# Attention on one Trainium2 core: value products in groups of four key tiles, one ring of three PSUM banks

## The reference

```python
h = relu(layernorm(x)); x = x + (adj @ h) @ W0 + b0
h = relu(layernorm(x)); x = x + norm_adj @ (h @ W1) + b1
h = relu(layernorm(x)); x = x + L2(h, mask = adj)     # attention, projection, o + layernorm(o)
h = relu(layernorm(x)); x = x + L3(h, mask = adj)     # attention, projection

def attention(h, mask):                 # for each of 8 heads of width 32
    s = scale * q @ k.T                 # 1024 x 1024
    p = softmax(where(mask, s, -inf))   # L3 adds -1e9 in place of -inf
    return (p @ v) @ Wo + bo
```

## Time and profile before

| | us |
|---|---|
| median of 3 runs | 2976.08 (2975.07 to 2977.13) |
| the profiled execution | 2974.42 |
| its span, first to last instruction | 2972.6 |

### The profile page before, as it was taken

The page is one execution under the profiler, slowest core; times in us unless marked ns, Lnnn a source line. Parts: engine busy times, 40 slices in busy tenths (PEclk is TensorE's granted clock), DMA queues, the critical chain, the costliest instruction groups (busy, mean ns, idle before and its releaser), DMA issues.

```text
span 2972.6 us, 59755 instructions
## 1 busy us (share of the span) xinstructions
PE 2906.1 (98%) x23872; PEld 2199.0 (74%) x23872; DVE 2401.1 (81%) x4427; ACT 2126.1 (72%) x3794; POOL 591.3 (20%) x538
## 2 busy tenths in 40 slices
PE   7999997999999999999999989999999999999998
PEld 6888886777777777777777767777777777777776
DVE  6776775879888888888888878888888787878786
ACT  3000002888888888888888878888888888888887
POOL 2222220105050504131322323010101010101000
PEclk9999998999999999999999999999999999999999
DMA  3001003323233233232323252323233332323232
GB/s 124 29 29 58 29 29 94 70 56 90 69 83 75 71 74 83 65 93 61 96 51 97 67 140 68 90 66 85 65 81 74 82 76 72 87 55 93 65 75 58
DMA packets 123588, 217.19 MB, mean 73 GB/s; under 512 B 20016, under 2 KB 88240, under 8 KB 123312
## 3 DMA queue, kind: packets, MB, share of 16 engines
q1 hardware_dynamic: 122160, 209.14, 28.4%
q0 software_dynamic: 1152, 4.19, 0.6%
HBM read 53.87 MB, written 25.17 MB: 27 GB/s over the span
## 4 chain that ended last, share of the span: by engine, by line
PE 79%; ACT 2%; DVE 1%; DMA 1%; issue 0%; ACTq 0%; DVEq 0%
PE t_pt_ps L732 32%; PE t_ot_ps L751 17%; PE t_s_ps L720 15%; PE t_g_ps L705 4%; PE t_g_ps L706 4%; PE t_g_ps L707 4%; PE t_g_ps L772 1%; PE t_g_ps L776 1%; PE t_g_ps L791 1%; ACT t_T L870 1%; ACT t_PT L875 1%; DMA mask<-in_adj 1%; DVE t_st_lo L957 0%; ACT t_st_hi L860 0%; ACT t_ot L881 0%
## 5 line engine op out<-in xcount | busy, mean ns | idle before, releaser
L939 DVE CUSTOM_DVE_ANT_0 t_T<-t_s_ps,mask 128x1024 f32<-128x1024 f32 x1024 | 1240.6, 1215 | 117.3 <-PE t_s_ps L720 112.5
L870 ACT ACTIVATE t_T<-t_T,t_low 128x1024 f32<-128x1024 f32 x1024 | 1178.8, 1151 | 43.1 <-DVE t_low L939 37.9
L732 PEld LDWEIGHTS t_pt_ps<-t_ident,t_T 128*128 128x128 f32 x8192 | 885.2, 141 | 325.7 <-issue 279.5
L732 PE MATMUL t_pt_ps<-t_ident,t_T 128*128 128x128 f32 x8192 | 1112.6, 279 | 6.3 <-DVE t_PT L1014 4.5
L875 ACT ACTIVATE t_PT<-t_pt_ps 128x512 f32<-128x512 f32 x1324 | 755.9, 596 | 317.9 <-PE t_pt_ps L732 306.7
L720 PE MATMUL t_s_ps<-t_k,t_q 128*128 128x512 f32 x2048 | 729.7, 437 | 8.3 <-DMA t_k<-t_st_lo 7.1
L1014 DVE COPY t_PT<-t_pt_ps 128x512 f32<-128x512 f32 x724 | 499.1, 689 | 196.6 <-PE t_pt_ps L732 194.0
L751 PE MATMUL t_ot_ps<-t_PT,shared 128*32 128x256 f32 x8192 | 549.4, 386 | 8.1 <-ACT t_PT L875 7.9
L751 PEld LDWEIGHTS t_ot_ps<-t_PT,shared 128*32 128x32 f32 x8192 | 215.1, 109 | 255.4 <-issue 128.0
L247 ACT ACTIVATE g_yT_hi<-g_ps 128x512 fp32r<-128x512 f32 x64 | 38.3, 598 | 400.5 <-PE g_ps L187 400.5
L720 PEld LDWEIGHTS t_s_ps<-t_k,t_q 128*128 128x128 f32 x2048 | 310.6, 192 | 9.3 <-DMA t_k<-t_st_lo 7.6
(11 more groups left out here) (185 smaller groups left out, 3158.1 us busy)
## 6 DMA issues: line engine op xcount, KB each, us to landing
t_q<-t_st_hi SPq DMA_DIRECT2D x256, 128.0 KB, 2.3
t_k<-t_st_hi SPq DMA_DIRECT2D x256, 128.0 KB, 2.4
t_k<-t_st_lo SPq DMA_DIRECT2D x256, 128.0 KB, 2.4
t_q<-t_st_lo SPq DMA_DIRECT2D x256, 128.0 KB, 2.4
shared<-x_after_graph_layers SPq DMA_DIRECT2D x8, 1024.0 KB, 6.5
t_xe<-x_after_graph_layers SPq DMA_DIRECT2D x32, 256.0 KB, 3.1
x_after_layer<-t_xe SPq DMA_DIRECT2D x32, 256.0 KB, 2.1
shared<-x_after_layer SPq DMA_DIRECT2D x8, 1024.0 KB, 6.8
```

Source lines behind the costliest of these rows:

```text
L732: last = nc.tensor.transpose(pt_ps[half][:, i * P:(i + 1) * P], T[u % RING][:, kt * P:(kt + 1) * P], ident[:])
L870: nc.scalar.activation(T[u % RING][:], T[u % RING][:], ACT.Exp, bias=low[:, u % RING:u % RING + 1], scale=-1.0, accum_out=rsum[:, u:u + 1] ...
L939: nc.vector.tensor_tensor_reduce(out=T[u % RING][:], in0=s_ps[u % 2][:], in1=mask[:, qt, :], scale=1.0, scalar=3.4e38, op0=ALU.add, op1=AL ...
```

## The change

- GROUP is 4: the value products of four key tiles follow each other, once in four units.
- The two banks for transposes and the one for blocks become one ring of three (`ring_ps`). `bank_plan` walks through the order in which TensorE fills banks, gives the fills (each half of a unit's transposes, each block) to banks 0, 1, 2, 0 ... and notes for each the bank and its count there. Each bank has a semaphore for filled and one for emptied; each fill waits for the emptying of the fill three before.
- All three engines' loops go over four units at a time, with an order written out. The halves of a unit's transposes are separate steps, partly half 1 first.
- The blocks stand in other units; ScalarE copies both halves in the 27 units of `BOTH_ON_ACT`.
- `mask3` of a tile is done just ahead of the first `masked` that uses it.
- SP's store of pair 1 stands behind the load of head 4, pair 2 behind head 5, pair 3 behind head 6.

```diff
-GROUP = 2
-EARLY = [(9, ("norm", 3)), (11, ("turn", 0)), (13, ("out", 0)), (15, ("turn", 1)), (17, ("out", 1)),
+GROUP = 4
+EARLY = [(10, ("norm", 3)), (13, ("turn", 0)), (16, ("out", 0)), (19, ("turn", 1)), (24, ("out", 1)),
          (26, ("turn", 2)), (28, ("out", 2)), (30, ("turn", 3)), (32, ("out", 3))]
-MID = [(18, ("qk", 1, 0, 0)), (20, ("qk", 1, 1, 0)), (22, ("qk", 1, 0, 1)), (24, ("qk", 1, 1, 1)),
-       (33, ("norm", 0)), (49, ("norm", 1)), (60, ("norm", 2))]
-NEXT = [(35, ("h", 0, 0)), (37, ("h", 0, 1)), (40, ("h", 1, 0)), (42, ("h", 1, 1)),
-        (44, ("v", 0)), (45, ("v", 1)), (47, ("v", 2)), (48, ("v", 3)),
-        (51, ("qk", 0, 0, 0)), (53, ("qk", 0, 1, 0)), (54, ("qk", 0, 0, 1)), (56, ("qk", 0, 1, 1))]
+MID = [(17, ("qk", 1, 0, 0)), (18, ("qk", 1, 1, 0)), (21, ("qk", 1, 0, 1)), (22, ("qk", 1, 1, 1)),
+       (34, ("norm", 0)), (43, ("norm", 1)), (59, ("norm", 2))]
+NEXT = [(35, ("h", 0, 0)), (37, ("h", 0, 1)), (38, ("h", 1, 0)), (39, ("h", 1, 1)),
+        (40, ("v", 0)), (44, ("v", 1)), (46, ("v", 2)), (47, ("v", 3)),
+        (49, ("qk", 0, 0, 0)), (50, ("qk", 0, 1, 0)), (51, ("qk", 0, 0, 1)), (53, ("qk", 0, 1, 1))]
+BOTH_ON_ACT = {2, 6, 11, 15, 17, 18, 19, 22, 23, 25, 26, 27, 30, 31, 33, 34, 35, 39, 42, 43, 45, 46, 47, 54, 55, 58, 62}
...
+def bank_plan(n_jobs):
...
+        for u in range(0, UNITS, GROUP):
+            order = [("T", job, u, 1), ("T", job, u, 0), ("T", job, u + 1, 0), ("T", job, u + 1, 1), ("B", job, u),
+                     ("T", job, u + 2, 1), ("T", job, u + 2, 0), ("B", job, u + 1), ("T", job, u + 3, 0), ("B", job, u + 2),
+                     ("T", job, u + 3, 1), ("B", job, u + 3)]
+            for key in order:
+                if key[0] == "T" or key[2] in table:
+                    use(key, n % BANKS)
+                    n += 1
...
         @block.tensor
...
+            def transposes(job, u, half):
+
+                if half == (1, 0, 1, 0)[u % GROUP]:
+                    pe.wait_ge(p_done, UNITS * job + u + 1)
+                b, n = place["T", job, u, half]
+                if n:
+                    pe.wait_ge(bank_freed[b], n)
...
-                for u in range(UNITS):
-                    if u + 2 < UNITS or after is not None:
-                        scores(job, u + 2, UNITS * job + u + 1)
...
-                    if u % GROUP == 0 and (u >= NT or before is not None):
+                for u in range(0, UNITS, GROUP):
+                    scores(job, u + 2)
+                    if u >= NT or before is not None:
                         for w in range(u, u + GROUP):
                             values(job, w)
-                    transposes(job, u)
+                    transposes(job, u, 1)
+                    scores(job, u + 3)
+                    transposes(job, u, 0)
+                    transposes(job, u + 1, 0)
+                    transposes(job, u + 1, 1)
+                    scores(job, u + 4)
+                    block_of(u)
+                    transposes(job, u + 2, 1)
+                    transposes(job, u + 2, 0)
+                    block_of(u + 1)
+                    scores(job, u + 5)
+                    transposes(job, u + 3, 0)
+                    block_of(u + 2)
+                    transposes(job, u + 3, 1)
+                    block_of(u + 3)
...
         @block.scalar
...
+                for u in range(0, UNITS, GROUP):
+                    exp(job, u + 1)
+                    if u % (2 * NT) == NT - GROUP and (u >= NT or before is not None):
+                        copy_ot(UNITS * job + u + GROUP - NT)
+                    exp(job, u + 2)
+                    copy_pt(job, u, 0)
+                    if u + 1 in BOTH_ON_ACT:
+                        copy_pt(job, u + 1, 1)
+                    hi_of(u, ("qk",))
+                    copy_pt(job, u + 1, 0)
+                    exp(job, u + 3)
+                    if u + 2 in BOTH_ON_ACT:
+                        copy_pt(job, u + 2, 1)
+                    copy_pt(job, u + 2, 0)
+                    hi_of(u, SHORT)
+                    hi_of(u + 1, SHORT + ("qk",))
+                    copy_pt(job, u + 3, 0)
+                    hi_of(u + 2, SHORT)
+                    exp(job, u + 4)
+                    hi_of(u + 2, ("qk",))
+                    hi_of(u + 3, SHORT)
+                    if u + 3 in BOTH_ON_ACT:
+                        copy_pt(job, u + 3, 1)
+                    hi_of(u + 3, ("qk",))
...
         @block.vector
...
-                if layer == 1 and job == B:
+                if job == B and u < NT:
+
+                    mask3(qt)
                     dve.wait_ge(mask3_done, qt + 1)
...
+                for u in range(0, UNITS, GROUP):
+                    masked(job, u + 2)
+                    stats_of(u, (0,))
+                    copy_pt(job, u)
+                    masked(job, u + 3)
+                    if u + 1 not in BOTH_ON_ACT:
+                        copy_pt(job, u + 1)
+                    finish_of(u, SHORT)
+                    stats_of(u, (1,))
+                    if u + 2 not in BOTH_ON_ACT:
+                        copy_pt(job, u + 2)
+                    masked(job, u + 4)
+                    finish_of(u, LONG)
+                    finish_of(u + 1, SHORT + LONG)
+                    masked(job, u + 5)
+                    if u + 3 not in BOTH_ON_ACT:
+                        copy_pt(job, u + 3)
+                    stats_of(u, (2, 3))
+                    finish_of(u + 2, SHORT + LONG)
+                    finish_of(u + 3, SHORT + LONG)
```

More of the change, by code:

```diff
@@ L426, with use @@
 LAST = [("norm", 3), ("turn", 0), ("turn", 1), ("out", 0), ("turn", 2), ("out", 1), ("turn", 3), ("out", 2), ("out", 3)]
-FIRST_QK = 8
+FIRST_QK = 7
 SHORT = ("h", "turn")
+LONG = ("qk", "v", "norm", "out")
 LN_STEP = 16
-PER_JOB = len(EARLY) + len(MID) + len(NEXT)
+BANKS = 3
 def blocks_of(first, more):
[L435 to L444, removed]
+    return dict((EARLY if not first else []) + MID + (NEXT if more else []))
+def bank_plan(n_jobs):
+    place, fills = {}, [0] * (BANKS + 1)
+    def use(key, bank):
+        place[key] = (bank, fills[bank])
+        fills[bank] += 1
+    for k in range(len(FIRST)):
+        use(("first", k), k % (BANKS + 1))
+    n = 0
+    for job in range(n_jobs):
+        table = blocks_of(job == 0, job + 1 < n_jobs)
+        for u in range(0, UNITS, GROUP):
[6 more added lines that the diff above has]
+                    n += 1
+    for k in range(len(LAST)):
+        use(("last", k), k % (BANKS + 1))
+    return place
 def attention_phase(nc, a, x_mid, x_mid2, out, mask, shared):
@@ L558, in attention_phase, with bank, key_of @@
         block = ctx.enter_context(nc.Block())
-        FIRST_BLOCKS = len(FIRST)
-        def block_at(job, k):
-            return PER_JOB * job + FIRST_BLOCKS - len(EARLY) + k
+        place = bank_plan(JOBS)
+        banks = ring_ps + [ot_ps]
+        def bank(key):
+            return banks[place[key][0]]
+        def key_of(job, what):
+            return next(("B", job, u) for u, w in EARLY + MID + NEXT if w == what)
         def layers_of(job):
@@ L641, in load_xe, with store @@
                              .rearrange("(t p) d -> p t d", p=P)).then_inc(xe_in[p], 16)
-            def store(job, layer, p, n):
+            def store(job, layer, p, key):
                 batch = job - B * layer
@@ L656, in body @@
             def body(job, layer, before, after):
-                table = blocks_of(before is None, after is not None)
-                at = {what: block_at(job, k) for k, what in table.values()}
                 if before is not None:
@@ L753, in values, with one_block @@
                 last.then_inc(av_done, 1)
[L755 to L768 removed]
+            def one_block(key, what, layer, job_of_h, needs=None, last=False):
+                if needs is not None:
+                    b, n = place[needs]
+                    pe.wait_ge(bank_freed[b], n + 1)
+                b, n = place[key]
+                if n:
+                    pe.wait_ge(bank_freed[b], n)
+                ps = banks[b]
                 kind = what[0]
@@ L838, in _ @@
             for k, what in enumerate(LAST):
-                one_block(tail_block(k), what, 1, None, k, True)
+                needs = {"norm": None, "turn": ("norm", 3), "out": ("turn", what[1])}[what[0]]
+                one_block(("last", k), what, 1, None, needs and ("last", LAST.index(needs)), True)
         @block.scalar
@@ L893, in _ @@
             for n, what in enumerate(FIRST):
[L894 removed]
+                hi_part(("first", n), what, 0, 0)
             weights_hi(1)
@@ L941, in masked, with finish_block @@
                                                accum_out=low[:, u % RING:u % RING + 1]).then_inc(t_done, 1)
-            def finish_block(n, what, layer, job, k=None, last=False):
-                kind, ps = what[0], bank(k)
+            def finish_block(key, what, layer, job, last=False):
+                kind, ps = what[0], bank(key)
+                b, n = place[key]
```

(4 more changed lines are left out.)

240 lines of the change are left out of this document (109 added, 131 removed).

## The result

| | before | after |
|---|---|---|
| median, us | 2975.57 (4 runs, 2973.66 to 2977.13) | 2865.69 (4 runs, 2863.30 to 2866.86) |
| the profiled execution | 2974.42 | 2864.98 |
| its span | 2972.6 | 2862.8 |

The ratio is 0.9628, with a 95% interval of 0.9617 to 0.964: 110 us faster, where 58 were forecast.

A forecast was written before the change was run, and what follows sets the result against it. TensorE was taken to set the pace, busy 152.46 of 153.23 us in a quiet job. Gains and losses 69 + 27 - 42 + 4 = 58 us gave a forecast of 2918 us, range 2876 to 2974.

The forecast's parts named there:

- Part 1: TensorE's value groups, GROUP 2 to 4: 254 fewer ways in and out of 32-wide values at 0.27 us each, 69 us gained.
- Part 2: Ring of three banks: transposes directly behind scores no longer wait for a bank, 0.09 us a unit, 27 us gained.
- Part 3: New waits of TensorE, ScalarE and VectorE in the new order: 2.6 us a job, 42 us lost.
- Units 36 to 39: Three h blocks come with the output copy; T(u+3,1) starts 0.65 us late, behind ScalarE's and VectorE's copies of h.
- The group at 16: At unit 16 the second block waits 0.3 us for VectorE to empty the first.
- Units 24 to 31: VectorE has "out", its statistics and the eight means there: 0.4 us lost.
- Part 4: ScalarE takes 91 of a job's 128 halves, not 83: 4 us more on ScalarE, 5.5 less on VectorE, hidden.
- Emptying binds: Rival, chance 0.20: ScalarE's copies and exponentials end last, each group waits 0.12 us more on average, giving 2949 us.
- Part 5: Turn to the second attention layer: moving the mask rework removes the second stall, about 7 us, less some 3; net 4 gained.
- the first stall: TensorE's 4.36 us wait for a head's load at the turn to the second attention layer, forecast to stay.
- 3 lost: Mask rework, 8 x 0.69 us, lies in VectorE's densest groups at the turn: 9.7 against 7.4, some 3 us lost.
- The rival on the slower side: The ring locks behind blocks, chance 0.14: blocks hold ring banks, so transposes, exponentials and copies are late together; 3017 us.

## Why the forecast was right in direction and too small

**Part 1 (69 us): the size holds, not as a part that stands alone.** V is 1.86 to 1.87 to the next start in all 254 groups (1.87 to 1.88 forecast); cut in two it costs 0.28 a group, and with the output copy out of the way 77 us in all. That a change of mode has a price is shown by this; that the price is one draining before the other starts fits the weight loads above, which aren't done ahead across the change. The Trainium skill, "TensorEngine Tiling (Array Packing)", Key Properties, says that changing the tiling mode drains TensorE, and these rows agree. But in the old order the same step loses 88 us.

**Part 2 (27 us): right.** S ahead of T went from 0.59 to 0.55 and T from 0.85 to 0.79, in the changed kernel and with the ring alone. The choice of 27 between zero and 27 was right: it was the bank.

**Part 3 (42 us lost): the term that failed.** It was mis-sized: the waits of the new order are 1.1 us a job, some 17 us in all, where 2.6 and 42 were put. Step by step:

- The output copy "shifts all by 0.4 and costs some 0.3": measured 0.05 (7.42 against 7.37). ScalarE's timeline around it, and in the quiet group:

```profile
1100.12 1.14 ACT L921 ACTIVATE t_T<-t_T,t_low 128x1024 f32<-128x1024 f32 x1
1101.29 0.60 ACT L933 ACTIVATE t_ot<-t_ot_ps 128x512 f32<-128x512 f32 x1
1101.79 1.15 ACT L921 ACTIVATE t_T<-t_T,t_low 128x1024 f32<-128x1024 f32 x1
1102.92 1.07 ACT L927 ACTIVATE t_PT<-t_ring_ps 128x512 f32<-128x512 f32 x2
...
1095.38 1.09 ACT L927 ACTIVATE t_PT<-t_ring_ps 128x512 f32<-128x512 f32 x2 [0.27 <-PE t_ring_ps L749]
```

  The group's S starts at 1098.65, so the copies start at 4.27, against 4.10 (1095.38 less 1091.28) without it: a shift of 0.17, not 0.4. The layout ignored that ScalarE stands idle for 0.27 just ahead of these copies, and that idle time takes more than half of the 0.5 us of the output copy. That uses the room up: one more copy there costs its whole 0.49 (the run with 35 units).
- Units 36 to 39, 0.65: measured 0.55, by the chain named: ScalarE's half of h at 37 late, then VectorE's, then the bank. That "three h blocks" make it is refuted, since with two the 0.55 stays. TensorE's row there:

```profile
1180.54 0.66 PE L749 MATMUL t_ring_ps<-t_ident,t_T 128*128 128x128 f32 x4 [0.32 <-DVE t_hT_lo L1020]
```

- The group at 16, 0.3: measured 0.2. Units 24 to 31, 0.4: measured 0.05 in two groups. Statistics and means on VectorE were covered.

**What the sum left out.** It took the old waits as standing. The kernel before had 1.0 us a job of them (the two rows of waits above are most of it), and the change removed them: 15 us. The quiet group came out 0.04 shorter than laid out, 0.6 a job, 10 us. Part 3 came out 25 smaller, and the turn gave 5 more. The last job gained only 2.6 (146.37 to 143.80) where the others gained 6.6, which takes 4 off; why is open. That is 51, against the 52 between the forecast of 58 and the measured 110.

**Part 4 (hidden): right,** with more room than I thought. Eight units more on ScalarE cost 6 us, eight fewer 38: VectorE was the tighter one, around the v block of unit 40. "Emptying binds" is refuted as a mean over groups: 13 of 16 groups lie within 0.11 of the floor. The rule of the Trainium skill, "TensorEngine Tiling (Array Packing)", PSUM Bottleneck, that the copy may bind, didn't decide here. It bears on the burst in the old order, where the copies did set the pace (158.8 us a job).

**Part 5 (4 us): the rework as priced, the first stall wrong; 9 measured.** In the kernel before, the two stalls with their slow restarts made jobs 7 and 8 longer by 6.9 and 6.6 us. The second is gone but for 0.43 and 0.54, as forecast. The "3 lost" to VectorE's dense groups came too: the first two groups of job 8 take 8.75 and 9.20 (S at 1679.44, 1688.19 and 1697.39) where 7.37 and 7.42 are usual, 3.2 us, and VectorE is at work without a gap from 1677.6 to 1696. What failed is "the first stays": it fell from 4.36 to 1.49, and with its restart from 6.9 to 1.8, which is the 5 us beyond the forecast. The last query block stands at 53 and not at 56, so the head's load can start earlier. The run with the old tables in the changed kernel bears this out: there the stall is 6.1. The early rework costs 8 in the new order, but done in fours and ahead of a stall that had become short, so this can't be set beside the 4 of the old order. The granted clock of job 7 is 1.00 where it was 0.96.

**The rival on the slower side** had the right mechanism for the wrong schedule. With the ring in the old order it cost 54 us, with the old tables in the new one 206. "The blocks shift by a few units: nothing" was the weakest sentence of the prediction. It came out well because tables and halves had been fitted to the ring, not because block places are free.

What stays open: how the 242 us divide between the order, the tables and `BOTH_ON_ACT` isn't a sum, since each was tried only from one side.

## What to carry to other kernels

A price read from the distance between starts (a mode switch, a bank's turn-round) held to 0.01 us, so such prices can be trusted; but parts of a schedule do not add, and one of them alone may cost what all together gain. Lay the new order out by hand together with what each engine stands idle for: an added copy costs only what that idle time doesn't take (0.05 for the first one here, 0.49 for the next), and waits of the old order that vanish belong in the sum. When a shared ring replaces own buffers, the places of its slow users, and the copies fitted around them, are part of the change and have a price, here 206 us. And read a group's time against its own floor: when a block moves out, its price goes with it, and only what is left over that floor tells whether a wait went too.

## What the runs showed that I had not expected

In the new order bursts had a best length: values of two tiles at a time (with the output copy moved), of four and of eight gave periods of 151.6, 146.6 and 158.0 us, though each longer one saves switches of 0.27. (Order and tables were fitted to four, so that four is best in general isn't shown.) The first loses the switches; the last loses 1.7 us in the quiet pair of groups, to the exponential and copies that come late behind 3.6 us of V. And the same burst of four went from a loss of 88 us to the best of all by what stands around it; that the split halves, with a fill for VectorE directly behind V, carry a part of this is shown (60 us), that the whole of it comes from shorter idle times of the emptying engines is not.
